# Score blocks of 64 by 64 tokens, with block-diagonal keys and values of head pairs, in a gated linear-attention and ternary feed-forward kernel

## The chip, the cores and the metric

The kernel runs on one core of a Trainium2 chip. The metric is device time in microseconds of one launch, median of the runs. Of the core's engines TensorE (PE in the rows; PEld is its weight load) multiplies, VectorE is DVE, ScalarE is ACT and GpSimd is POOL. SyncE (SP) only issues DMA transfers here; its rows are marked SPq. Names such as hid_a or score_b are PSUM banks.

## What is computed

x is 8 batches of 1024 tokens by 256 features, with 16 heads of 16 dimensions. Cut to what matters:

```python
xn = layernorm(x)
Q, K, V = (xn @ W.T).reshape(B, L, 16, 16)            # for Wq, Wk, Wv
g = clip(sigmoid(xn per head @ gw.T), 1e-6)
Gc = exp(clip(cumsum(log g), -30, 30)) + 1e-6
R = silu(K @ sw.T)
S = cumsum(outer(K, V) * R / Gc) * Gc                 # over tokens, per head
attn = einsum(Q, S) @ Wo.T
ffn = ternary(w_proj) applied to relu(ternary(w_fc) applied to xn + low-rank term) ** 2
out = x + attn + ffn
```

The cumulative sum over tokens is computed by chunks of 128 tokens: inside a chunk as masked scores (K times Q, kept where the key's token is not later than the query's) times V * R / Gc, and across chunks by a state that is carried.

## The kernel before

Work goes by units of 256 tokens (two chunks c = 0, 1 of 128), four units (u) to a batch (b), 32 in all. Each engine has its own program, written out by hand: a `prologue()` for the start, then `slot(b, u)` 27 times, then an `epilogue()`. In a slot, `nxt` is the unit one ahead, `after` two ahead, and the front of the pipeline works three and four ahead. Engines meet through semaphores alone, and each runs its list strictly in the order written, so the order in the slots is the schedule. SP issues all steady transfers on one queue, also in its written order.

The path of a unit: x is loaded and normalised (DVE, ACT, POOL), turned by a transposing DMA (`turn_tokens`), and multiplied into queries (L2272), keys (L2294), values and gates (L2313), and hidden features (L2418, L2420), whose squares go through `projected` (L2447). Queries and keys are kept as pairs of f16 halves, high and low.

- **Scores** (L2346). The contraction of 128 rows holds two heads of 16 dimensions times the four products of high and low parts. `stack_queries` (L492, 8 transfers) writes q_diag, in which head s of a pair has its own columns and zeros below the other head; `turn_keys` (L558, one transposing transfer) and `stack_keys` (L571, 4 transfers) write k_stack. One matmul has 128 keys of a pair as weights and moves 256 columns: 128 queries for each of two heads. Four groups g of two matmuls make a chunk, in banks score_a and score_b by turns.
- **Mask** (L1829, DVE): each group of 128x512 from PSUM to SBUF, times the causal triangle. A group's bank is free only after that.
- **Values** (L2384): v_pad holds each head's weighted values beside zeros, 32 columns wide. Sixteen f32 matmuls per chunk, each 128 columns of one head's scores, go to four 32-column strips of the array, four side by side. The rows count two entries for one f32 matmul. v_pad is written by POOL, `weigh_values` (L719), twice per unit.
- **State**: `state_updates` (L2361), in the same 32-column form with 64 moving columns; DVE adds it (L1843, L1847), POOL spreads it (`diagonal_state`, L746), and `carried` (L2397) adds its part to attn_bank.
- `attn_projected` (L2462) ends a unit's output; `cumulate` (L2326) makes the running sums of log gates, with 64 moving f16 columns.

In the prologue POOL turns the feed-forward weights into ternary halves (L821, L829, L836, L842), and ACT first sums their absolute values (L1230).

## Time and profile before

| what | value |
|---|---|
| median of 3 runs | 637.78 us (637.02 to 638.42) |
| span of the profiled execution, which is also its time | 637.8 us |
| PE busy | 620.1 us (97%) |
| DVE, ACT, POOL busy | 528.7, 443.3, 387.3 us (83%, 70%, 61%) |
| DMA queue q1, share of 16 engines' time | 68.4% |
| chain that ended last, on PE | 89% |

The first and last instruction are 637.8 us apart, within 0.1 us of the median, so the sums are made against 637.8. A matmul's own duration in a row (273 ns for 256 columns) overlaps with its neighbours'; what it costs is the distance between the starts of two. The chain that ended last merges equal pieces and shows that distance.

### The profile page before, as it was taken

How to read it: one execution, taken by the hardware profiler on the slowest of the kernel's cores; microseconds unless marked ns; L12 is line 12 of the kernel's file. 1: busy time of each engine (PE TensorE's matmuls, PEld its weight loads, DVE VectorE, ACT ScalarE, POOL GpSimd, SP SyncE). 2: the span in 40 equal slices, each digit the busy share in tenths (PEclk: the TensorE clock that was granted, in tenths of full speed). 3: DMA queues.
4: the chain of work that ended last, by engine and by line, in shares of the span. 5: the costliest groups of instructions: out<-in, count | busy, mean ns of one | idle time of the engine just before them, and what ended most of it. 6: DMA issues, size and time to landing. Idle time of an engine off the chain costs nothing.

```text
span 637.8 us, 21397 instructions
## 1 busy us (share of the span) xinstructions
PE 620.1 (97%) x7710; PEld 545.8 (86%) x7710; DVE 528.7 (83%) x1241; ACT 443.3 (70%) x1036; POOL 387.3 (61%) x505
## 2 busy tenths in 40 slices
PE   7789999999999999999999999999999999999997
PEld 7667888888888888888888888888888888888886
DVE  7678978899888888898789988798988887897863
ACT  4568766677776667776666767775777766677664
POOL 4896666555656665556566565655565665666454
PEclk7689999999999999999999999999999999999999
DMA  9446656886796887866788887668887477775631
GB/s 303 104 97 107 131 106 147 136 145 131 139 147 109 141 138 130 143 133 128 121 145 132 132 146 145 125 106 136 134 143 151 117 137 131 135 130 124 115 54 51
DMA packets 190361, 83.31 MB, mean 131 GB/s; under 512 B 121888, under 2 KB 189728, under 8 KB 190256
## 3 DMA queue, kind: packets, MB, share of 16 engines
q1 hardware_dynamic: 188016, 79.32, 68.4%
q10 hardware_dynamic: 2240, 2.62, 1.3%
q8 instruction: 62, 1.02, 0.8%
q14 instruction: 43, 0.35, 0.2%
HBM read 12.43 MB, written 8.39 MB: 33 GB/s over the span
## 4 chain that ended last, share of the span: by engine, by line
PE 89%; POOL 4%; issue 2%; DMA 2%; SPq 1%; DVE 1%; ACT 1%; ACTq 0%; DVEq 0%; POOLq 0%
PE y_bank L2447 17%; PE attn_bank L2384 9%; PE hid_b L2418 8%; PE hid_a L2418 8%; PE front_b L2313 7%; PE y_bank L2462 7%; PE front_b L2272 7%; PE front_a L2294 6%; PE attn_bank L2397 4%; PE score_a L2346 4%; PE score_b L2346 4%; PE hid_b L2420 2%; PE hid_a L2420 2%; PE score_b L2361 2%; POOL sq_l L821 1%
## 5 line engine op out<-in xcount | busy, mean ns | idle before, releaser
L1871 DVE TENSOR_TENSOR sq_l<-relu_sq,sq_h 128x512 f16<-128x512 f32 x128 | 115.8, 907 | 3.7 <-ACT relu_sq L1162 2.6
L2447 PE MATMUL y_bank<-wproj_t,sq_h 128*128 128x256 f16 x504 | 117.0, 273 | 0.2 <-DVE sq_l L1871 0.2
L2447 PE MATMUL y_bank<-wproj_t,sq_l 128*128 128x256 f16 x504 | 117.0, 273 | 0.0
L1829 DVE TENSOR_TENSOR masked<-score_a,shapes_sb 128x512 f32<-128x512 f32 x128 | 88.2, 689 | 29.6 <-PE score_a L2346 29.0
L1829 DVE TENSOR_TENSOR masked<-score_b,shapes_sb 128x512 f32<-128x512 f32 x128 | 87.5, 684 | 14.0 <-PE score_b L2346 13.7
L746 POOL TENSOR_TENSOR state_diag<-state,state_mask 128x256 f32<-128x256 f32 x56 | 46.8, 836 | 70.7 <-DVE state L1847 34.3
L1153 ACT ACTIVATE sq_h<-relu_sq 128x512 f16<-128x512 f32 x128 | 79.0, 618 | 0.9
L1162 ACT ACTIVATE relu_sq<-relu_sq 128x512 f32<-128x512 f32 x128 | 78.7, 616 | 0.8 <-DVE sq_l L1871 0.7
L2418 PE MATMUL hid_b<-xt,wfc_t 128*128 128x256 f16 x512 | 73.6, 273 | 0.0
L2418 PE MATMUL hid_a<-xt,wfc_t 128*128 128x256 f16 x512 | 73.4, 273 | 0.1
L672 POOL TENSOR_SCALAR xn<-x_sb,neg_mean,rstd 128x256 f32<-128x256 f32 x64 | 42.3, 662 | 50.1 <-DVE rstd L1723 49.9
L679 POOL TENSOR_TENSOR xn<-xn 128x512 f16<-128x512 f32 x31 | 35.9, 1159 | 58.7 <-ACT xn L985 58.7
L2384 PE MATMUL attn_bank<-masked,v_pad 128*32 128x128 f32 x2048 | 68.4, 274 | 0.6 <-POOL v_pad L719 0.6
L719 POOL TENSOR_TENSOR v_pad<-vg,write 128x256 f32<-128x256 f32 x64 | 38.6, 624 | 42.8 <-DVE write L1818 42.8
L2313 PE MATMUL front_b<-wvg_h,xt 128*128 128x304 f16 x256 | 61.6, 299 | 3.1 <-DVE wvg_l L1561 2.8
L1142 ACT ACTIVATE relu_sq<-hid_b,hid_scale 128x256 f32<-128x256 f32 x128 | 53.6, 473 | 13.4 <-PE hid_b L2420 13.2
L2384 PEld LDWEIGHTS attn_bank<-masked,v_pad 128*32 128x32 f32 x2048 | 52.9, 110 | 7.2 <-issue 6.1
L1047 ACT ACTIVATE vg<-front_b 128x304 f32<-128x304 f32 x64 | 27.5, 430 | 42.1 <-PE front_b L2313 42.1
L1001 ACT ACTIVATE q<-front_b 128x512 f16<-128x512 f32 x32 | 19.1, 596 | 53.3 <-PE front_b L2272 51.8
L766 POOL TENSOR_TENSOR attn_l<-attn,attn_h 128x256 fp32r<-128x256 f32 x64 | 55.8, 874 | 0.2
L1142 ACT ACTIVATE relu_sq<-hid_a,hid_scale 128x256 f32<-128x256 f32 x128 | 52.5, 460 | 4.3 <-PE hid_a L2420 4.3
L2447 PEld LDWEIGHTS y_bank<-wproj_t,sq_h 128*128 128x128 f16 x504 | 49.3, 98 | 6.2 <-DVE sq_l L1871 0.5
(224 smaller groups left out, 1656.9 us busy)
## 6 DMA issues: line engine op xcount, KB each, us to landing
q_diag<-q SPq DMA_DIRECT2D x256, 64.0 KB, 2.8
k_stack<-k SPq DMA_DIRECT2D x128, 128.0 KB, 4.3
x_sb<-in_x SPq DMA_DIRECT2D x32, 256.0 KB, 3.2
out_y<-y_both SPq DMA_DIRECT2D x31, 256.0 KB, 3.2
relu_sq<-in_w_fc ACTq DMA_DIRECT2D x1, 1024.0 KB, 11.5
pj_nat<-in_w_proj ACTq DMA_DIRECT2D x1, 1024.0 KB, 14.2
y_both<-in_w_qk ACTq DMA_DIRECT2D x1, 512.0 KB, 5.1
w_stage<-in_w_qkvz_t SPq DMA_DIRECT2D x1, 512.0 KB, 6.7
```

What stands on the lines that cost most here:

```text
L746: nc.gpsimd.tensor_tensor(state_diag[:].rearrange("p t (g s e) -> p (t g) s e", s=2, e=HD), lanes.unsqueeze(2).to_broadcast([P, KT * 4, 2, ...
L766: nc.gpsimd.tensor_tensor(attn_l[:, u % 2, c], attn[:, c], attn_h[:, u % 2, c].bitcast(F32), ALU.subtract).then_inc(attn_l_done, 1)
L1142: last = nc.scalar.activation(relu[:, n, half], hid_bank[n][:, half], ACT.Relu, scale=hid_scale[:, 2 * q + i:2 * q + i + 1])
L1153: nc.scalar.activation(sq_h[:, q], relu[:, q % 2], ACT.Square).then_inc(sq_h_done, 1)
L1162: nc.scalar.activation(sq[:, n], relu[:, n], ACT.Square).then_inc(sq_done, 1)
L1829: nc.vector.tensor_tensor(masked[:, c, g].rearrange("p (h n) -> p h n", h=4), score_bank[g % 2][:].rearrange("p (h n) -> p h n", h=4), cau ...
L1871: nc.vector.tensor_tensor(sq_l[:, q], sq[:, n], sq_h[:, q], ALU.subtract).then_inc(sq_l_done, 1)
L2313: last = mm(front_b[:, 0:VG], part[:, at, c, t], w[:, t], start=(n == 0), stop=(n == 3 * KT - 1), skip_group_check=True)
L2346: last = mm(score_bank[g % 2][:, i * 2 * P:(i + 1) * 2 * P], k_stack[:, par, g, c, i], q_diag[:, par, 2 * g + i, :, c * P:(c + 1) * P], st ...
L2384: last = mm(attn_bank[32 * q:32 * q + 32, (c * KT + half) * P:(c * KT + half + 1) * P], v_pad[:, par, c, 8 * half + 2 * q + odd], masked[: ...
L2418: mm(place, wfc_t[:, t, j * P:j * P + P], part[:, at, :, t], start=(t == 0 and part is xt_h), stop=False)
L2447: last = mm(out_part(b, u, c), part[:, q, at:at + P], wproj_t[:, 2 * q + i], start=(q == i == n == 0 and (c == 0 or last_of_all(b, u))), s ...
```

## The change

Scores are cut into causal blocks of 64 keys. The weights of one matmul now hold 64 keys of the two heads of a pair, block-diagonal (k_diag: keys of one head beside zeros, below them zeros beside the keys of the other), and q_stack has both heads' dimensions in its rows with the queries moved once. Rows are stacked four apart (`n:P:PART`). Per chunk there are three waves in place of four groups: waves 0 and 1 multiply keys 0 to 63 by all 128 queries (4 matmuls of 128 columns each), wave 2 multiplies keys 64 to 127 by queries 64 to 127 alone (8 matmuls of 64 columns). The quarter in which all keys are later than the queries is not computed. The values' weights (v_pair) hold both heads of a pair, 64 keys each; half of a head's rows must change their partitions for it. POOL's `keep_rows` writes those that stay, DVE's new `move_rows` those that move, and v_all keeps plain weighted values for the state update. Every engine's order is written anew.

```diff
@@ -65,7 +65,10 @@
 STATES = NU * CH - 1
 PART = 4
 XBUFS, TBUFS = 6, 5
-Q_DMAS, K_DMAS = 2 * PART, PART
+Q_DMAS, K_DMAS = PART, 2 * PART
+SUB = P // 2
+WAVES = 3
+ROW = CH * KT * 2 * P
...
         k_tok16 = sb("k_tok16", [P, 2, CH, D], F16)
-        k16 = sb("k16", [P, 2, CH, KT, P], F16)
-        k_stack = sb("k_stack", [P, 2, PAIRS // KT, CH, KT, P], F16)
-        q_diag = sb("q_diag", [P, 2, PAIRS, 2, UNIT], F16)
+        k16 = sb("k16", [P, 2, CH * KT * 2, 2, SUB], F16)
+        k_diag = sb("k_diag", [P, 2, PAIRS // KT * ROW + SUB], F16)
+        q_stack = sb("q_stack", [P, 2, PAIRS, UNIT], F16)
...
-        v_pad = sb("v_pad", [P, 2, CH, H, 2 * HD])
-        masked = sb("masked", [P, CH, 4, 512])
+        v_all = sb("v_all", [P, 2, CH, D])
+        v_pair = sb("v_pair", [P, 2, CH, 2, PAIRS, 2 * HD])
+        masked = sb("masked", [P, CH, WAVES, 512])
+        causal_two = sb("causal_two", [P, P])
...
+        def keys_of(par, g, c, t, s):
+
+            at = g * ROW + ((c * KT + t) * 2 + s) * P
+            return k_diag[:, par, at:at + P]
...
-                    sp.wait_ge(score_full, upto(pb, pu, 4 * CH, 4 * CH - 1))
-                if b == 0 and u < 2:
-                    sp.wait_ge(q_cleared[par], 2)
-                for s in range(2):
-                    for n, part in enumerate((0, 1, 0, 1)):
-                        rows = slice(32 * n + HD * s, 32 * n + HD * (s + 1))
-                        sp.dma_start(q_diag[rows, par, :, s, :],
-                                     q16[64 * s:64 * s + 64, part]).then_inc(q_stacked[par], 16)
+                    sp.wait_ge(score_full, upto(pb, pu, WAVES * CH, WAVES * CH - 1))
+                for n, part in enumerate((0, 1, 0, 1)):
+                    sp.dma_start(q_stack[n:P:PART, par], q16[:, part]).then_inc(q_stacked[par], 16)
...
-                sp.dma_start(k16[:].rearrange("p s c t n -> p (s c t) n"),
-                             k_tok16[:].rearrange("p s c d -> p (s c d)"),
-                             transpose=True).then_inc(k_turned[u % 2], 16)
+                if first_of_all(b, u):
+                    sp.wait_ge(k_cleared, 2)
+                for h in range(2):
+                    sp.dma_start(k16[:].rearrange("p s (x h) z n -> p (s x) h z n", h=2)[:, :, h, 0],
+                                 k_tok16[SUB * h:SUB * h + SUB].rearrange("p s c d -> p (s c d)"),
+                                 transpose=True).then_inc(k_turned[u % 2], 16)
...
-                for n, part in enumerate((0, 0, 1, 1)):
-                    sp.dma_start(k_stack[32 * n:32 * n + 32, par], k16[:, part]).then_inc(k_stacked[par], 16)
+                    sp.wait_ge(score_full, upto(pb, pu, WAVES * CH, WAVES * CH - 1))
+                if b == 0 and u < 2:
+                    sp.wait_ge(k_cleared, 2)
+                for s in range(2):
+                    to = k_diag[:, par, SUB * s:SUB * s + PAIRS // KT * ROW].rearrange("p (g n) -> p g n", n=ROW)
+                    for n, part in enumerate((0, 0, 1, 1)):
+                        sp.dma_start(to[SUB * s + n:SUB * s + SUB:PART],
+                                     k16[64 * s:64 * s + 64, part]).then_inc(k_stacked[par], 16)
 
             def slot(b, u):
-                nxt, prev, after = unit_after(b, u, 1), unit_after(b, u, -1), unit_after(b, u, 2)
-                load(*unit_after(b, u, 4))
+                nxt, after = unit_after(b, u, 1), unit_after(b, u, 2)
+                stack_queries(*after)
                 turn_tokens(*unit_after(b, u, 3))
                 stack_keys(*after)
+                store(*unit_after(b, u, -2))
+                spread_totals(*after)
                 turn_decays(*nxt)
+                load(*unit_after(b, u, 5))
                 turn_z(*after)
-                spread_totals(*after)
-                store(*unit_after(b, u, -2))
-                stack_queries(*unit_after(b, u, 3))
                 turn_keys(*unit_after(b, u, 3))
...
-                    pool.wait_ge(attn_full, carried_upto(pb, pu, CH - 1))
-                val = vg[:, par, c, 0:D].rearrange("p (g s e) -> p g s e", s=2, e=HD)
-                fac = heads_bc(write[:, par, c], HD).rearrange("p (g s) e -> p g s e", s=2)
+                    pool.wait_ge(updates_done, upto(pb, pu, 1, 0))
+                val = vg[:, par, c, 0:D].rearrange("p (h e) -> p h e", e=HD)
+                nc.gpsimd.tensor_tensor(v_all[:, par, c].rearrange("p (h e) -> p h e", e=HD), val,
+                                        heads_bc(write[:, par, c], HD), ALU.mult).then_inc(v_all_done, 1)
+
+            def keep_rows(b, u):
+
+                if not exists(b):
+                    return
...
+                    pool.wait_ge(values_done, upto(pb, pu, CH, CH - 1))
                 if b == 0 and u < 2:
                     pool.wait_ge(v_cleared[u], 1)
-                nc.gpsimd.tensor_tensor(v_heads(par, c, 0, H), val, fac, ALU.mult).then_inc(v_pad_done, 1)
+                for s in range(2):
+                    rows = slice(SUB * s, SUB * s + SUB)
+                    nc.gpsimd.tensor_tensor(block_of(par, rows, s, s), heads_of(vg[:, par, :, 0:D], rows, s),
+                                            weights_of(par, rows, s), ALU.mult).then_inc(v_kept_done, 1)
+
+                    pool.wait_ge(v_kept_done, upto(b, u, 2, s))
...
             def slot(b, u):
                 nxt, prev, after = unit_after(b, u, 1), unit_after(b, u, -1), unit_after(b, u, 2)
                 diagonal_state(*nxt, 0)
-                attn_high(b, u, 1)
+                attn_low(b, u, 0)
                 residual(*prev)
+                attn_low(b, u, 1)
+                sums_before(*after)
                 normalise(*unit_after(b, u, 4), 0)
-                attn_low(b, u, 1)
+                normalise(*unit_after(b, u, 4), 1)
+                xt_low(*unit_after(b, u, 4))
                 diagonal_state(*nxt, 1)
-                normalise(*unit_after(b, u, 4), 1)
-                sums_before(*after)
-                xt_low(*unit_after(b, u, 4))
+                keep_rows(*after)
                 weigh_values(*after, 0)
+                attn_high(*nxt, 0)
                 weigh_values(*after, 1)
-                attn_high(*nxt, 0)
+                attn_high(*nxt, 1)
                 split_decay(*after)
-                attn_low(*nxt, 0)
...
             def prologue():
-                rstd_guess(0, 0)
-                causal_taken()
-                ident_taken()
-                columns_high(0)
-                first_high()
-                columns_high(1)
                 fc_sums(0)
                 fc_sums(1)
+                rstd_guess(0, 0)
+                proj_sums()
+                columns_high(0)
                 rstd_guess(0, 1)
-                keys(0, 0)
-                keys_high(0, 0)
-                queries_high(0, 0)
-                queries_full(0, 0)
+                first_high()
                 values_high()
                 z_norms()
+                columns_high(1)
...
+            def move_rows(b, u, s):
+
+                if not exists(b):
+                    return
+                par, rows = u % 2, slice(SUB * s, SUB * s + SUB)
+                to = slice(SUB * (1 - s), SUB * (1 - s) + SUB)
+                dve.wait_ge(write_done, upto(b, u, 1, 0))
...
+                nc.vector.tensor_tensor(block_of(par, to, s, 1 - s), heads_of(vg[:, par, :, 0:D], rows, 1 - s),
+                                        weights_of(par, rows, 1 - s), ALU.mult).then_inc(v_moved_done, 1)
+
             def mask(b, u, c, g):
...
-                nc.vector.tensor_tensor(masked[:, c, g].rearrange("p (h n) -> p h n", h=4),
-                                        score_bank[g % 2][:].rearrange("p (h n) -> p h n", h=4),
-                                        causal_sb.unsqueeze(1).to_broadcast([P, 4, P]), ALU.mult).then_inc(mask_done, 1)
+                width = P if g < KT else SUB
+                shape = causal_two[:, 0:width].unsqueeze(1).to_broadcast([P, 512 // width, width])
+                nc.vector.tensor_tensor(masked[:, c, g].rearrange("p (h n) -> p h n", n=width),
+                                        score_bank[(WAVES * c + g) % 2][:].rearrange("p (h n) -> p h n", n=width),
+                                        shape, ALU.mult).then_inc(mask_done, 1)
...
-                if started(upto(b, u, 4 * CH, 4 * c + g) - 2):
-                    pe.wait_ge(mask_done, upto(b, u, 4 * CH, 4 * c + g) - 2)
-                for i in range(2):
-                    last = mm(score_bank[g % 2][:, i * 2 * P:(i + 1) * 2 * P],
-                              k_stack[:, par, g, c, i],
-                              q_diag[:, par, 2 * g + i, :, c * P:(c + 1) * P], start=True, stop=True)
+                if started(upto(b, u, WAVES * CH, WAVES * c + g) - 2):
+                    pe.wait_ge(mask_done, upto(b, u, WAVES * CH, WAVES * c + g) - 2)
+                to = score_bank[(WAVES * c + g) % 2]
+                if g < KT:
+                    for i in range(PAIRS // KT):
+                        last = mm(to[:, i * P:(i + 1) * P], keys_of(par, i, c, g, 0),
+                                  q_stack[:, par, KT * i + g, c * P:(c + 1) * P], start=True, stop=True)
+                else:
+                    for t in range(KT):
+                        for i in range(PAIRS // KT):
+                            at = (t * (PAIRS // KT) + i) * SUB
+                            last = mm(to[:, at:at + SUB], keys_of(par, i, c, t, 1),
+                                      q_stack[:, par, KT * i + t, c * P + SUB:(c + 1) * P], start=True, stop=True)
                 last.then_inc(score_full, 1)
...
-                pe.wait_ge(mask_done, upto(b, u, 4 * CH, 4 * CH - 1))
+                pe.wait_ge(mask_done, upto(b, u, WAVES * CH, WAVES * CH - 1))
+                pe.wait_ge(v_all_done, upto(b, u, CH, CH - 1))
...
-                pe.wait_ge(mask_done, upto(b, u, 4 * CH, 4 * c + 3))
+                pe.wait_ge(mask_done, upto(b, u, WAVES * CH, WAVES * c + WAVES - 1))
                 for half in range(KT):
-                    for odd in range(2):
+                    for later in range(2):
                         for q in range(4):
-                            pair = KT * q + half
-                            at = (pair % 2 * 2 + odd) * P
-                            last = mm(attn_bank[32 * q:32 * q + 32, (c * KT + half) * P:(c * KT + half + 1) * P],
-                                      v_pad[:, par, c, 8 * half + 2 * q + odd],
-                                      masked[:, c, pair // 2, at:at + P],
-                                      start=(c == half == odd == 0), stop=False, skip_group_check=True)
+                            at = (c * KT + half) * P
+                            if later:
+                                cols = (4 * half + q) * SUB
+                                place, moving = slice(at + SUB, at + P), masked[:, c, KT, cols:cols + SUB]
+                            else:
+                                place, moving = slice(at, at + P), masked[:, c, half, q * P:q * P + P]
+                            last = mm(attn_bank[32 * q:32 * q + 32, place], v_pair[:, par, c, later, 4 * half + q], moving,
+                                      start=(c == half == later == 0), stop=False, skip_group_check=True)
                 last.then_inc(values_done, 1)
```

PE, one steady slot, before: from the end of the hidden layer to the first score groups.

```order
L2420 MATMUL hid_b<-z_stack,rank_w 128x256
L2384 MATMUL attn_bank<-masked,v_pad 32x128 x16
L2361 MATMUL score_b<-v_pad,k_tok 32x64 x16
L2384 MATMUL attn_bank<-masked,v_pad 32x128 x16
L2397 MATMUL attn_bank<-q_t,state_diag 128x128 x2
L2272 MATMUL front_b<-xt,wqk 128x256 x12
```

PE, the same place in the changed kernel (L2460 values, L2432 state updates, L2471 carried, L2388 cumulate, L2334 queries, L2356 keys).

```order
L2460 MATMUL attn_bank<-masked,v_pair 32x64 x4
L2432 MATMUL score_b<-v_all,k_tok 32x64 x16
L2471 MATMUL attn_bank<-q_t,state_diag 128x128 x2
L2388 MATMUL front_a<-log,causal 128x64
L2334 MATMUL front_b<-xt,wqk 128x256 x12
L2460 MATMUL attn_bank<-masked,v_pair 32x128 x4
L2460 MATMUL attn_bank<-masked,v_pair 32x64 x4
L2460 MATMUL attn_bank<-masked,v_pair 32x128 x4
L2460 MATMUL attn_bank<-masked,v_pair 32x64 x4
L2356 MATMUL front_a<-wqk,xt 128x256 x12
```

The second chunk's values, which stood right behind the state updates, now stand alone between the queries and the keys; half of the value matmuls are 64 columns wide.

SP, one steady slot, before (from the token load on):

```order
L466 DMA x_sb<-in_x 128x2x256
L504 DMA_TRANSPOSE xt<-xn 128x8x128
L571 DMA k_stack<-k 32x4x512 x4
L531 DMA_TRANSPOSE turned_halves<-decay_halves 128x8x128
L519 DMA_TRANSPOSE z_stack<-z 128x2x128
L546 DMA totals<-chunk_sums 128x1x32
L477 DMA out_y<-y_both 128x2x256
L492 DMA q_diag<-q 16x8x256 x8
L558 DMA_TRANSPOSE k<-k_tok 128x8x128
```

SP, one steady slot of the changed kernel:

```order
L505 DMA q_stack<-q 32x4x512 x4
L516 DMA_TRANSPOSE xt<-xn 128x8x128
L590 DMA k_diag<-k 16x4x1024 x8
L494 DMA out_y<-y_both 128x2x256
L558 DMA totals<-chunk_sums 128x1x32
L543 DMA_TRANSPOSE turned_halves<-decay_halves 128x8x128
L483 DMA x_sb<-in_x 128x2x256
L531 DMA_TRANSPOSE z_stack<-z 128x2x128
L573 DMA_TRANSPOSE k<-k_tok 128x8x64 x2
```

Eight query transfers became four, four key transfers eight (of twice the elements in sum, zeros included), and one transposing transfer two of half the rows.

ACT, the first work behind the table load, before, and then in the changed kernel (L1278 sums the feed-forward weights, L1019 and L1021 begin a unit's reciprocal deviation, L1287 sums the projection's weights, L1251 takes the high half of the query and key columns):

```order
L973 ACTIVATE log_var<-var_eps 128x2
L975 ACTIVATE guess<-log_var 128x2
L1087 ACTIVATE causal<-shapes_sb 128x128
L1208 ACTIVATE ident<-shapes_sb 128x128
L1209 ACTIVATE ident<-shapes_sb 128x128
L1203 ACTIVATE wqk<-q_t 128x2x256
```

```order
L1278 ACTIVATE sq_h,fc_scale<-relu_sq 128x256 x8
L1019 ACTIVATE log_var<-var_eps 128x2
L1021 ACTIVATE guess<-log_var 128x2
L1287 ACTIVATE y_both,pj_scale<-pj_nat 128x1024 x2
L1251 ACTIVATE wqk<-q_t 128x2x256
```

The first unit's guess now stands behind the sums of the feed-forward weights.

## Rows read from the trace of the kernel before

**Rows 1.** Page, parts 1 and 2: busy time; granted TensorE clock in tenths.

```profile
PE 620.1 (97%) x7710; PEld 545.8 (86%) x7710; DVE 528.7 (83%) x1241; ACT 443.3 (70%) x1036; POOL 387.3 (61%) x505
...
PEclk7689999999999999999999999999999999999999
```

**Rows 2.** Busy time by stretch: window, length, PE, PEld, DVE, ACT, POOL, clock, DMA share, GB/s.

```profile
52.00:137.60 85.60, 84.25 (x1125) 73.37 (x1117) 71.81 (x168) 62.20 (x147) 52.58 (x73) 1.00 0.63 127
...
285.50:433.00 147.50, 147.50 (x1883) 130.78 (x1875) 128.48 (x295) 105.92 (x248) 89.08 (x118) 1.00 0.76 132
```

**Rows 3.** Timeline of PE: state updates of two units four apart: start, length.

```profile
285.47 0.34 PE L2361 MATMUL score_b<-v_pad,k_tok 128*32 128x64 f32 x11
...
359.43 0.28 PE L2361 MATMUL score_b<-v_pad,k_tok 128*32 128x64 f32 x6
```

**Rows 4.** Chain that ended last, one unit: start, length, what.

```profile
303.33 1.01 PE attn_bank L2384 x32
304.34 0.45 PE score_b L2361 x32
304.78 0.87 PE attn_bank L2384 x32
305.65 0.64 PE attn_bank L2397 x4
...
308.48 0.45 PE attn_bank L2397 x4
308.93 0.03 PE front_a L2326
...
311.14 0.22 PE score_a L2346 x2
```

**Rows 5.** Timeline of PE in the prologue: f16 matmuls with 128x128 weights each.

```profile
35.58 0.22 PE L2208 MATMUL y_bank<-ident,sq_h 128*128 128x128 f16 x1 [2.52 <-issue]
...
36.02 0.19 PE L2326 MATMUL front_a<-log,causal 128*128 128x64 f16 x1
36.05 0.22 PE L2208 MATMUL attn_bank<-ident,sq_h 128*128 128x128 f16 x1
```

**Rows 6.** Weight loads of the scores: busy us, mean ns of one.

```profile
L2346 PEld LDWEIGHTS score_b<-q_diag,k_stack 128*128 128x128 f16 x256 | 24.7, 98 | 5.2 <-DVE masked L1829 1.0
```

**Rows 7.** Timeline of SP's issues, one unit: start, length.

```profile
320.45 2.54 SPq L571 DMA_DIRECT2D k_stack<-k  x4
...
324.77 1.17 SPq L519 DMA_TRANSPOSE z_stack<-z  x1
327.71 0.53 SPq L546 DMA_DIRECT2D totals<-chunk_sums  x1
...
328.98 5.16 SPq L492 DMA_DIRECT2D q_diag<-q  x8
...
338.58 1.91 SPq L571 DMA_DIRECT2D k_stack<-k  x3
```

**Rows 8.** One line's DMA issues: ns min/median/max.

```profile
L558 SPq DMA_TRANSPOSE k<-k_tok x32: 1245/1272/2722, 20.1 to 595.3; - x32
```

**Rows 9.** DMA share and rate of a stretch in which the key stack is written.

```profile
28.90:31.40 2.50, 2.50 (x27) 2.00 (x27) 1.72 (x10) 1.08 (x4) 2.50 (x4) 0.79 0.95 201
```

**Rows 10.** Page, part 5: mask (DVE) and weighted values (POOL).

```profile
L1829 DVE TENSOR_TENSOR masked<-score_a,shapes_sb 128x512 f32<-128x512 f32 x128 | 88.2, 689 | 29.6 <-PE score_a L2346 29.0
...
L719 POOL TENSOR_TENSOR v_pad<-vg,write 128x256 f32<-128x256 f32 x64 | 38.6, 624 | 42.8 <-DVE write L1818 42.8
```

**Rows 11.** Timeline of POOL in the prologue.

```profile
9.15 1.10 POOL L672 TENSOR_SCALAR xn<-x_sb,neg_mean,rstd 128x256 f32<-128x256 f32 x2 [4.40 <-DVE rstd L1723]
...
17.37 3.63 POOL L829 TENSOR_SCALAR sq_h<-relu_sq,fc_scale 128x256 f16<-128x256 f32 x4 [3.50 <-DVE fc_inv L1582]
```

**Rows 12.** Timeline of ACT in the prologue: the first sum of feed-forward weights.

```profile
13.38 0.42 ACT L1230 ACTIVATE sq_h<-relu_sq 128x256 f16<-128x256 f32 x1 [0.74 <-DMA relu_sq<-in_w_fc]
```

**Rows 13.** Timeline of PE in the prologue: the first unit's values.

```profile
51.52 1.08 PE L2384 MATMUL attn_bank<-masked,v_pad 128*32 128x128 f32 x32 [0.59 <-POOL v_pad L719]
```

870 lines of the change are left out of this document (442 added, 428 removed).

## The prediction

> **What bounds the kernel now.** I read the page's busy line and clock line first [rows 1]: PE is busy 97% of the span, and after the first slices the clock stands at full. Busy PE is not yet a bound, since matmuls overlap in that line, so the second view is the busy time by stretch [rows 2]: from 285.5 to 433 us PE has no idle time at all, and between 52 and 137.6 only 1.35 us. The third is the chain that ended last [rows 4], in which one PE piece follows the next without a wait. Two units four apart start 359.43 - 285.47 = 73.96 us apart [rows 3], so a unit takes 18.49 us, and that is the sum of PE's pieces. Whatever PE work disappears from the slot shortens the kernel, as long as the others keep up: DVE works 128.48/147.50 x 18.49 = 16.1 us per unit, POOL 11.2 us, and the DMA engines 0.76 x 18.49 = 14.1 us [rows 2]. The first 51.5 us are another regime: the first values wait for POOL [rows 13].
>
> **Scores.** Before, 16 matmuls of 256 columns per unit at 0.22/2 = 0.11 us [rows 4], 1.76 us. After, 16 matmuls of 128 columns and 16 of 64, each with its own 128x128 f16 weights. The prologue has the first form: eight steps from 35.58 to 36.02, 0.055 us each [rows 5]. Of the second form it has one at a time: `cumulate`, 64 columns, is followed 0.03 us later by a matmul with other weights [rows 5], and the same 0.03 stands in the steady chain [rows 4]. So 16 x 0.055 + 16 x 0.03 = 1.36 us, a gain of 0.40 us per unit. Eight of the short form in a row are nowhere in this trace. If each needs the step of the 128-column form after all, 0.055 us, the gain is 0.00; it cannot be much below 0.03. I take 0.03, because in both places the next weights had to be loaded beside a 64-column matmul.
>
> **Values.** Before, 0.87 us per chunk for 32 entries of 128 columns, 0.027 each [rows 4]. The state updates are the same 32-column form with 64 columns: 0.45 us for 32 entries, 0.014 each [rows 4]. After, a chunk is 16 entries of each: 0.435 + 0.225 = 0.66 us. Gain 0.21 per chunk, 0.42 us per unit.
>
> **What the new order costs on PE.** The f32 work on 32-column strips now stands in two blocks per unit, the second chunk's values alone between queries and keys. Entering such a block costs 1.01 - 0.87 = 0.14 us, and leaving it at most 0.64 - 0.45 = 0.19 us [rows 4], part of which may be the carried matmul's own f32 weights. A second block costs 0.14 to 0.33 us; I take 0.24. PE's balance is 0.40 + 0.42 - 0.24 = 0.58 us per unit, a unit of 17.91 us, and 32 x 0.58 = 18.6 us in all.
>
> **DVE and POOL.** DVE loses two masks of 0.69 us per unit and gains two `move_rows` of 256 elements on half the partitions: no such row exists; a mask of 512 elements (0.69) bounds it from above, nothing from below, and 0.4 is near half. DVE then needs 16.1 - 1.38 + 0.8 = 15.5 of 17.9 us, the share it has now. POOL gains two `keep_rows`, at most 0.62 each as the 256-element product of today [rows 10]: 12.4 of 17.9 us. Both stay below PE. The waits for v_kept, v_moved and v_all come in the slot before the one that reads them. Behind `keep_rows`, which waits for the write factors, stand only `weigh_values`, `attn_high` and `split_decay` on POOL, which need them or come later. I charge zero to 5 us over the whole run for brushes between neighbours, and take 1.3.
>
> **SP's queue and the transfers.** This cover is thin. From 320.45 to 338.58 the queue stands still only between the end of the issue at 324.77 and the one at 327.71, 1.77 us [rows 7]; 16.36 us are issuing. The number of plain issues stays 15 (8 + 4 + 3 before, 4 + 8 + 3 after), and they cost by count, not by bytes: 5.16/8 = 0.645 us for 64 KB, 2.54/4 = 0.635 us for 128 KB. But the keys' transpose becomes two issues. If each costs what the whole does, 1.27 us [rows 8], SP needs 17.6 us of a unit of 17.9. If it divides, nothing is added; I take the whole, the nearest row. The bytes of the key stack double, 0.5 MB more per unit, at the 201 GB/s of a stretch full of such writes 2.6 us [rows 9]: the DMA engines would be busy 16.7 of 17.9 us. In the new slot `stack_keys` stands ahead of `spread_totals`, which waits for a sum that PE's `cumulate` makes early in its slot; so the keys are issued some 6 us ahead of their first score group and have room for a landing that is late by one or two.
>
> **The start.** ACT now sums the feed-forward weights before the first unit's guess. Their data come at 13.38 us and eight sums follow [rows 12], and POOL puts the first 3.63 us of ternary work, at 17.37, ahead of the first xn, which stood at 9.15 [rows 11]. The first unit's tokens are some 12 us later. Most of this does not reach the end, since the first values waited for POOL, at 51.52 [rows 13]. But POOL gets work in front of those values that it had done in idle time: 1.10 for xn [rows 11], two subtractions of 512 elements at twice 0.62, two `keep_rows` at 0.62, and a copy of about 1: 5.8 us. PE in turn takes other work ahead of them, one hidden quarter, queries and keys of unit 2, 10 x 0.11 + 12 x 0.11 + 12 x 0.11 = 3.7 us. 2 us remain. SP has to fill the pipeline at 17.6 us per unit, and I add 2 for that: +4 us, between 0 and 8. The end I leave as it is.
>
> **The sum.** 637.8 - 18.6 + 4 + 1.3 = 624.5 us.
>
> **The rivals.**
> (A) The forecast, 624.5; 618 to 630 with the bounds above.
> (B) The start costs nothing and PE is the only bound: 637.8 - 18.6 = 619.
> (C) SP's queue or the landings hold PE a little, a unit of 18.2: (18.2 - 17.9) x 29 = 8.7 us more, 633. For it: 0.3 us of room. Against it: a queue with less than PE's period catches up.
> (D) A 64-column matmul with 128x128 weights steps by 0.055: 0.025 x 16 x 32 = 12.8 us more, 637, no change. Against it: the 0.03 of [rows 4, 5].
> (E) Slower: SP's queue becomes the bound. Its place is `turn_keys`, now two issues, and the stack of twice the bytes behind them. It decides once SP needs more than 18.4 us, 2.0 more than now: two transposes at the 2.72 us that the longest took [rows 8] would do it, or a DMA load over 18.4 us, where I have 16.7. A unit of 19.0 gives 623.2 + 1.1 x 29 = 655.
> (F) Slower: weights in a row do not hide behind short matmuls. A load's record lasts 98 ns [rows 6]; if that were the step, 32 x 0.098 = 3.14 us stand for 1.36, and 624.5 + 1.78 x 32 = 681. Against it: loads of the same 98 ns step by 55 ns in [rows 5].
> The Trainium skill ("TensorE: Matmul & The Clock Gate", section "Back-to-back issue gap") speaks for something like F: it gives about 81 ns for a 128-column matmul in a stream with weight loads, and calls the 56 ns of a lone one too low. By that page, an estimate, the scores would take at least 32 x 0.081 = 2.6 us per unit, some 40 us more than I have, and the kernel would be near 664. The eight in a row of [rows 5] step by 55 ns, so I go by the trace.
>
> **How the numbers follow.** A 0.56, B 0.10, C 0.14, D 0.07, E 0.10, F 0.03. A measurement of this kernel can tell about 0.2% from no change, 1.3 us. Faster: A, B, C and a part of D, 0.82. Within 0.2%: the middle of D, 0.04. Slower: E, F and the rest of D, 0.14. The range from 616 to 638 takes in A to D and leaves out E, F and a few in a hundred below.
>
> **What would show it.** In the profile of the changed kernel: score groups of four 128-column matmuls and of eight 64-column ones both stand as pieces of 0.22 to 0.24 us in the chain (0.44 for the second is D); values of a chunk stand as 0.66 us, 0.80 where they enter; PEld's idle time ahead of the values' loads doubles; units four apart are 71.6 us apart; the first values start near 57 us. If SP's list of waits is nearly empty and PE waits for key, query or token transfers, it is C or E. If the period is right and the end late, my start was too cheap. The forecast is wrong as a whole if DVE or POOL, not PE, stands in the chain.

## The result, and the profile after

| | before | after |
|---|---|---|
| median, runs side by side | 638.26 us (636.64 to 642.45, 20 runs) | 641.41 us (637.86 to 647.18, 20 runs) |
| ratio | | 1.0045, 95% interval 1.0028 to 1.0061 |
| span of the profiled execution | 637.8 us | 636.1 us |

The change makes the kernel 0.45% slower, 3.2 us, where 624.5 us was forecast. The profile of after is that of the fastest of its 20 runs: its time is 637.86, 1.8 us above its span, and in every later run here the time lies 1.8 us above the span. So the profiled execution of before, with a span of 637.8, took some 639.6, which is 1.3 above its median, while that of after lies 3.5 below its own. My sum started at 637.8, which is within 0.5 us of the median and 1.8 too low for the profile. A comparison of the two profiles therefore makes the change look better than it is: -1.7 us, where the medians say +3.2.

The page of after, parts 1, 2 (clock) and 3 (the plain queue: packets, MB, share of the 16 DMA engines), and the shares of the chain that ended last:

```profile
PE 602.5 (95%) x8222; PEld 525.4 (83%) x8222; DVE 557.2 (88%) x1239; ACT 442.0 (69%) x1036; POOL 427.8 (67%) x569
...
PEclk8799999999999999999999999999999999999999
...
q1 hardware_dynamic: 172816, 96.16, 61.9%
...
PE 64%; DVE 8%; issue 7%; SPq 7%; POOL 6%; DMA 4%; ACT 2%; DVEq 0%; ACTq 0%; POOLq 0%
```

PE is busy 17.6 us less than before [rows 1], so its work did become smaller. But it has a chain in which it holds 64% only; issue time, SP's queue and POOL have come in. The busy time by stretch (columns as in [rows 2]):

```profile
57.00:146.00 89.00, 82.10 (x1199) 69.91 (x1200) 74.81 (x167) 59.47 (x137) 59.71 (x81) 1.00 0.65 155
146.00:290.80 144.80, 143.95 (x2024) 126.50 (x2019) 135.38 (x295) 105.73 (x249) 97.21 (x135) 1.00 0.68 166
290.80:437.00 146.20, 144.36 (x2027) 126.50 (x2020) 136.33 (x295) 105.91 (x250) 97.66 (x135) 1.00 0.70 164
437.00:583.00 146.00, 144.45 (x2024) 126.43 (x2016) 135.25 (x291) 106.13 (x250) 99.67 (x136) 1.00 0.67 166
```

In the first 89 us PE stands idle for 6.9 us, where before it had 1.35 idle us in a like stretch [rows 2]; behind that, 0.85 to 1.8 us per 8 units, where before had none up to 433 us and 1.3 in the last 150. The share of the DMA engines is not the cause: it fell from 0.76 to 0.70, though the bytes rose. DVE works 93% of the stretch.

The timeline of PE (start, length, what) gives the starts of the state updates of units 1, 6 and 31:

```profile
57.28 0.32 PE L2432 MATMUL score_b<-v_all,k_tok 128*32 128x64 f32 x8
...
146.00 0.29 PE L2432 MATMUL score_b<-v_all,k_tok 128*32 128x64 f32 x8
...
601.30 0.29 PE L2432 MATMUL score_b<-v_all,k_tok 128*32 128x64 f32 x8
```

The same points stood before at 52.41, 137.56 and 601.52. Between the two profiles that makes +4.87 us up to the first, +3.57 over five units, -8.66 over the 25 units of the loop (455.30 for 463.96 us, 18.21 us a unit for 18.56), -1.61 for unit 32 and +0.09 behind it: -1.7 in all, as the spans say. The loop gives back 0.35 us a unit, not 0.58, and 8.4 us go before it settles.

SP's timeline of one unit (same columns) shows what is new:

```profile
296.53 0.57 SPq L483 DMA_DIRECT2D x_sb<-in_x  x1
...
298.46 2.53 SPq L573 DMA_TRANSPOSE k<-k_tok  x2
301.08 3.15 SPq L505 DMA_DIRECT2D q_stack<-q  x4
304.33 1.27 SPq L516 DMA_TRANSPOSE xt<-xn  x1
305.70 5.05 SPq L590 DMA_DIRECT2D k_diag<-k  x8
310.80 1.05 SPq L494 DMA_DIRECT2D out_y<-y_both  x1
311.95 0.54 SPq L558 DMA_DIRECT2D totals<-chunk_sums  x1
312.60 1.28 SPq L543 DMA_TRANSPOSE turned_halves<-decay_halves  x1
313.93 1.21 SPq L483 DMA_DIRECT2D x_sb<-in_x  x1
315.23 1.17 SPq L531 DMA_TRANSPOSE z_stack<-z  x1
316.50 3.93 SPq L573 DMA_TRANSPOSE k<-k_tok  x2
```

From one `turn_keys` to the next, 298.46 to 316.50, there is no pause: 18.04 us of work, where [rows 7] had 16.36 and a pause. Added up from the traces over the 25 slots of the loop (issues with the gaps of 0.05 to 0.1 us between them), the queue's work is 17.9 us a slot on average and up to 19.6, with 0.3 of pauses; before it was 16.2 with 2.3 of pauses. The lists of waits (us in total, times, longest) follow, SP's and then POOL's. SP's is nearly empty in the loop, and on POOL the sums over earlier units now wait for their totals, 29 times (before: 10.6 us in all):

```profile
SPq L516 <- POOL xn L703: 21.1, 1, 21.1
...
SPq L573 <- DVE k_tok L1782: 5.0, 8, 1.5
...
SPq L558 <- DVE chunk_sums L1822: 1.7, 2, 1.1
```

```profile
POOL attn_h L801 <- DVE attn L1923: 68.7, 29, 3.1
POOL before L719 <- DMA totals<-chunk_sums: 54.6, 29, 5.6
```

The wait of 21.1 us is one, in the prologue. Before, the loop's waits were 34.5 us in 28 for `chunk_sums` and 20.7 in 18 for `z`.

PE's own list of waits names no transfer in the loop, only DVE, in small pieces. The chain of after shows how a late queue still reaches PE, here ahead of one of the two longest units, 19.6 us:

```profile
441.68 3.96 DMA totals<-chunk_sums
...
445.71 0.23 POOL before L719
...
449.22 0.69 DVE masked L1894
...
449.95 0.40 PE score_b L2410 x4
```

The new order has the totals of log gates behind the eight key writes and the store on the queue. When they land late, POOL's sums are late, then DVE's work on them and the masks behind it, and PE waits for a mask. The other long unit, 19.5 us, has the same chain.

### The profile page after: what moved, and what is told of

Read it like the earlier page. It is cut to its first block, busy times and chain, and to the rows that moved or that the text cites. A ratio compares the mean times of both kernels' runs of the same rounds, so it can differ in the third digit from the quotient of the medians.

```text
span 636.1 us, 22704 instructions
## 1 busy us (share of the span) xinstructions
PE 602.5 (95%) x8222; PEld 525.4 (83%) x8222; DVE 557.2 (88%) x1239; ACT 442.0 (69%) x1036; POOL 427.8 (67%) x569
## 3 DMA queue, kind: packets, MB, share of 16 engines
q1 hardware_dynamic: 172816, 96.16, 61.9%
## 4 chain that ended last, share of the span: by engine, by line
PE 64%; DVE 8%; issue 7%; SPq 7%; POOL 6%; DMA 4%; ACT 2%; DVEq 0%; ACTq 0%; POOLq 0%
PE y_bank L2521 12%; PE hid_a L2492 6%; PE front_b L2375 6%; PE hid_b L2492 6%; PE y_bank L2536 6%; PE attn_bank L2460 6%; PE front_a L2356 5%; PE front_b L2334 5%; PE attn_bank L2471 3%; SPq L590 3%; DMA totals<-chunk_sums 3%; DVE masked L1894 2%; PE score_b L2410 2%; DMA relu_sq<-in_w_fc 2%; PE score_a L2410 2%
## 5 line engine op out<-in xcount | busy, mean ns | idle before, releaser
L1936 DVE TENSOR_TENSOR sq_l<-relu_sq,sq_h 128x512 f16<-128x512 f32 x128 | 111.1, 870 | 2.4 <-ACT sq_h L1201 1.8
L1210 ACT ACTIVATE relu_sq<-relu_sq 128x512 f32<-128x512 f32 x128 | 80.2, 628 | 41.5 <-DVE sq_l L1936 41.4
L801 POOL TENSOR_TENSOR attn_h<-attn,ones 128x256 fp32r<-128x256 f32 x64 | 56.8, 888 | 70.3 <-DVE attn L1923 68.7
L1894 DVE TENSOR_TENSOR masked<-score_b,causal_two 128x512 f32<-128x512 f32 x96 | 65.5, 683 | 2.3 <-PE score_b L2410 1.5
L1894 DVE TENSOR_TENSOR masked<-score_a,causal_two 128x512 f32<-128x512 f32 x96 | 65.2, 680 | 0.7 <-PE score_a L2410 0.3
L2460 PEld LDWEIGHTS attn_bank<-masked,v_pair 128*32 128x32 f32 x2048 | 45.2, 109 | 12.5 <-issue 11.9
L2460 PE MATMUL attn_bank<-masked,v_pair 128*32 128x128 f32 (+1 forms) x2048 | 55.3, 249 | 0.1
L2521 PEld LDWEIGHTS y_bank<-wproj_t,sq_l 128*128 128x128 f16 x504 | 49.3, 98 | 5.0
L2492 PEld LDWEIGHTS hid_a<-xt,wfc_t 128*128 128x128 f16 x512 | 47.7, 98 | 6.6 <-issue 1.1
L2492 PEld LDWEIGHTS hid_b<-xt,wfc_t 128*128 128x128 f16 x512 | 47.9, 98 | 5.2
```

Of the source, the lines that this page charges most:

```text
L801: nc.gpsimd.tensor_tensor(attn_h[:, u % 2, c], attn[:, c], ones[:].unsqueeze(1).to_broadcast([P, KT, P]), ALU.mult).then_inc(attn_h_done, 1)
L1210: nc.scalar.activation(sq[:, n], relu[:, n], ACT.Square).then_inc(sq_done, 1)
L1894: nc.vector.tensor_tensor(masked[:, c, g].rearrange("p (h n) -> p h n", n=width), score_bank[(WAVES * c + g) % 2][:].rearrange("p (h n) -> ...
L1936: nc.vector.tensor_tensor(sq_l[:, q], sq[:, n], sq_h[:, q], ALU.subtract).then_inc(sq_l_done, 1)
L2460: last = mm(attn_bank[32 * q:32 * q + 32, place], v_pair[:, par, c, later, 4 * half + q], moving, start=(c == half == later == 0), stop=Fa ...
L2492: mm(place, wfc_t[:, t, j * P:j * P + P], part[:, at, :, t], start=(t == 0 and part is xt_h), stop=False)
```

## The experiments

**The theories.** S: SP's queue, full since the key transpose is two issues, sets the pace of the changed loop. V: DVE, 93% busy, sets it. L: the transfers land late, though the queue has room. F: the order of the start costs time of its own. P: PE's pieces are not as short as I summed. The chain already speaks against P. One unit of it:

```profile
309.28 0.45 PE score_b L2432 x32
309.72 0.64 PE attn_bank L2471 x4
...
311.70 0.80 PE attn_bank L2460 x32
312.50 1.42 PE front_a L2356 x12
...
317.20 0.22 PE score_a L2410 x4
...
319.30 0.23 PE score_a L2416 x8
```

**One more small transfer per unit, in each kernel.** The same edit in both:

```diff
                 turn_keys(*unit_after(b, u, 3))
+                sp.dma_start(spare_in[:, nth(b, u)], shapes[0:16, 0:8]).then_inc(gates_loaded, 16)
```

> The changed kernel with one more transfer at the end of each of SP's 27 slots: 16 rows of 32 bytes into a tile that nothing reads. Theory S (SP's issue queue is the bound of the changed kernel: its trace shows SP without idle time between issues and units 18.1 to 18.2 us apart): each extra issue costs its 0.6 to 0.65 us, so 27 x 0.63 = 17 us, 655 to 661 us. Theory V (VectorE, 93% busy in the steady stretches, is the bound) and theory L (landings are late, the queue has room): nothing, 641 us within 2.

> The kernel before with the same extra transfer in each of SP's 27 slots. All theories: SP stands still for about 1.8 us per unit there, so 0.63 us more is free: 638 us within 1.5. If it costs 5 us or more, the queue already counted before the change, and theory S would be too simple.

Measured: the changed kernel 657.06 us (653.91 to 660.9, 4 runs; ratio to before 1.0268, 1.0227 to 1.0309), 15.6 above its own 641.4 (14.2 when each is taken by its ratio to before): 0.53 to 0.58 us for each of 27 issues, one whole issue each. The kernel before 641.34 (10 runs; 1.0039, 1.0012 to 1.0066), 2.3 us for the same 27. So after has no slack in this queue and before has most of 0.6 us. The first is as S expected, and V and L expected nothing of it; the second is nearly as expected (it was to be free). S stands, but this does not say what filled the queue.

**The second transpose alone, in the kernel before.**

```diff
-                sp.dma_start(k16[:].rearrange("p s c t n -> p (s c t) n"),
-                             k_tok16[:].rearrange("p s c d -> p (s c d)"),
-                             transpose=True).then_inc(k_turned[u % 2], 16)
+                for h in range(2):
+                    sp.dma_start(k16[:].rearrange("p s c t n -> p (s c t) n")[:, :, P // 2 * h:P // 2 * h + P // 2],
+                                 k_tok16[P // 2 * h:P // 2 * h + P // 2].rearrange("p s c d -> p (s c d)"),
+                                 transpose=True).then_inc(k_turned[u % 2], 16)
...
```

Those who wait for the turned keys count two transfers per unit in place of one; nothing else differs.

> The kernel before with the keys' transposing transfer cut into two of half the rows, as the change does. It prices the second transpose by itself. Theory S: 1.2 to 1.3 us more issue time per unit, which eats most of the 1.8 us of idle time: 638 to 642 us, SP's waits shrink by about 35 us in sum. If half a transpose costs half, the waits stay as they were.

Measured: 660.9 us (657.77 to 664.16, 4 runs; 1.0335, 1.0297 to 1.0373), 22 us slower. This was a miss, and the most useful one. SP's waits and PE's first:

```profile
SPq L546 <- DVE chunk_sums L1780: 22.8, 24, 3.5
...
SPq L519 <- DVE z L1801: 8.5, 11, 2.1
```

```profile
PE front_b L2273 <- DMA xt<-xn: 17.5, 16, 2.5
```

```profile
DVE stats L1681 <- DMA x_sb<-in_x: 21.3, 23, 3.0
```

The queue still waits for 22.8 + 8.5 us there, and yet PE now waits for the turned tokens, 16 times, and DVE's statistics for x, 23 times, which the kernel before did once (1.3 us) and 6 times (5.1 us). The chain of that run has one of these waits, and the timeline of the queue what lies around it:

```profile
318.63 5.25 DMA xt<-xn
...
323.93 1.48 PE front_b L2273 x12
```

```profile
318.63 1.24 SPq L504 DMA_TRANSPOSE xt<-xn  x1
319.97 3.01 SPq L572 DMA_DIRECT2D k_stack<-k  x4
323.07 1.26 SPq L531 DMA_TRANSPOSE turned_halves<-decay_halves  x1
324.60 1.17 SPq L519 DMA_TRANSPOSE z_stack<-z  x1
327.06 0.53 SPq L546 DMA_DIRECT2D totals<-chunk_sums  x1
...
328.33 6.52 SPq L492 DMA_DIRECT2D q_diag<-q  x8
334.95 2.54 SPq L559 DMA_TRANSPOSE k<-k_tok  x2
```

PE stands idle for 1.8 us until the tokens issued at 318.63 have landed. From 289 to 324.3, almost two slots, the queue has no gap of more than 0.1 us: the eight query writes took 6.4 us in each, where [rows 7] have 5.16, and the key writes 3.96 and 3.01 for 2.54. The pause, 325.8 to 327.1, comes only behind PE's wait; it stands ahead of the totals, which wait for PE's sums. In the next slot the queries follow without a wait. The landing itself is not slower than in the kernel before, 4.0 us in the median against 3.9; the issue comes late. So the queue is full for a slot or two, holds PE, and waits for PE afterwards, and its pauses in other slots do not pay for that. I had read a pause per unit as room for as much work: some 0.6 us nearly fitted, 1.27 did not. The two halves cost 2.54 together, and each 1264 ns in the median of 64, the whole's 1272.

**The same transpose taken out of the changed kernel, and DVE relieved.** Two omissions from the fifth unit on, alone and together (the counts of those who wait for the transpose are adapted):

```diff
-                for h in range(2):
+                for h in range(2 if nth(b, u) < 4 else 1):
...
```

```diff
-                nc.vector.tensor_tensor(block_of(par, to, s, 1 - s), heads_of(vg[:, par, :, 0:D], rows, 1 - s),
-                                        weights_of(par, rows, 1 - s), ALU.mult).then_inc(v_moved_done, 1)
+                if nth(b, u) < 4:
...
+                else:
+                    nc.vector.tensor_tensor(block_of(par, to, s, 1 - s)[:, 0, 0, 0:2],
...
```

> The changed kernel without the second of its two key transposes per unit from the fifth unit on (half of the keys' rows stay those of earlier units, so that the output differs): the transfer queue loses some 1.5 us of its 18 us per unit. It is the mirror of the second transpose added to the kernel before, which cost 22 us. Theory S (queue): the loop falls to TensorE's own 17.99 us per unit and the last of the start with it, time 633 to 637, and the queue shows waits again of about 1.5 us per unit. Theory V (VectorE): no change beyond 1 us, 640 to 642. Theory B: part of it, 637 to 640.

> The changed kernel with the work of VectorE's two value moves per unit (64x256, 0.52 us each) left out from the fifth unit on: they write two elements instead, so that the output differs; nothing else moves. VectorE loses 0.9 us of its 16.9 busy us per unit of 18.1. Theory S (the transfer queue is the bound of the changed kernel's loop): no change beyond 1 us, 640 to 642. Theory V (VectorE, 93 per cent busy, is what holds TensorE since the change): the loop comes down from 18.2 to 18.3 us a unit to TensorE's own 18.0, time 634 to 637. Theory B (each of the two is near the bound and delays TensorE in its turn): part of it, 638 to 640.

> Both of the two last omissions at once (second key transpose and the work of the value moves, each from the fifth unit on). Theory S: as the omission of the transpose alone. Theory V: as the omission of the moves alone. Theory B (both near their bounds): lower than either, loop at 17.99 us per unit throughout, time 631 to 635, some 3 us below the better of the two.

| | median us | ratio to before |
|---|---|---|
| one transpose | 631.59 (630.41 to 636.45, 5 runs) | 0.9900, 0.9866 to 0.9934 |
| no value moves | 640.33 (638.4 to 644.84, 10 runs) | 1.0034, 1.0010 to 1.0058 |
| both | 630.61 (628.51 to 631.87, 4 runs) | 0.9878, 0.9843 to 0.9914 |

Against after's 641.41 and 1.0045 the transpose is worth 9.3 us by the ratios and 9.8 by the medians, more than S expected. DVE's 0.9 us per unit give 0.7 to 1.1, alone or on top of the transpose, and the intervals of these pairs overlap: no gain of DVE is clear of the noise. This decides for S against V, and leaves B at most 1 us. The kernel with one transpose, its page and PE by stretch:

```profile
PE 76%; DVE 7%; issue 5%; POOL 4%; DMA 3%; SPq 3%; ACT 2%; ACTq 0%; DVEq 0%; POOLq 0%
```

```profile
57.00:146.00 89.00, 84.47 (x1250) 72.61 (x1249) 76.97 (x172) 61.14 (x140) 61.24 (x83) 1.00 0.67 160
...
290.80:437.00 146.20, 145.84 (x2062) 128.66 (x2061) 137.62 (x299) 106.43 (x251) 102.93 (x138) 1.00 0.65 159
```

PE is busy 145.84 of 146.20 us in the second, with DVE at 94% beside it: in this order DVE can be this full and hold PE for 0.4 us at most. The 25 units take 450.82 us, 18.03 each, with a cycle of 18.10, 18.10, 17.88 and 17.74 us where nothing waits, 17.96 on average. That is PE's own time for a unit; with both omissions the 25 units take 449.13, 17.97 each.

**Loads and stores on ACT's queue.**

```diff
                 stack_keys(*after)
-                store(*unit_after(b, u, -2))
                 spread_totals(*after)
                 turn_decays(*nxt)
-                load(*unit_after(b, u, 5))
```

with `store_behind` behind `z_high` and `load_ahead` behind `decay_exp` in ACT's slot, the same transfers on ACT's queue.

> The changed kernel with the steady loads of x and stores of the output issued from ScalarE's queue in place of SP's (ScalarE is 69% busy): SP has 1.2 to 1.9 us less per unit. Theory S: units fall from 18.2 to PE's own 17.9 us and the pipeline fills faster, 628 to 635 us. Theory V: VectorE does the same work, 641 us or more. Theory L: bytes and landings are the same, 641 us.

Measured: 640.43 us (12 runs; 1.0019, 1.0000 to 1.0038), 1 to 1.7 us under after, not 6 or more. Two issues less per unit, and no gain to speak of: S missed here, and V and L come nearer. DVE's waits of that kernel:

```profile
DVE stats L1737 <- DMA x_sb<-in_x: 5.3, 5, 3.4
```

In after that wait stood once, 3.5 us, ahead of the first unit, and one of these five is the same; the four in the loop make 1.9 us together. The queue has pauses again, 1.6 us a slot, and yet the 25 units take 457.35 us, 8.5 more than PE's own time. PE waits for masks there, 4.3 us in 9 and 3.3 in 4 (after: 2.2 in 6 and 2.3 in 2). So a queue with room is not enough; what holds this kernel was not found. The next runs moved the stores alone, with the start order as a second factor.

**The start order of before, and the stores alone.** `after_early` puts the order ahead of the first unit back on all engines; on POOL it reads

```diff
-                fc_highs(0)
                 normalise(0, 0, 0)
                 normalise(0, 0, 1)
                 columns_low(0)
-                fc_lows(0)
+                columns_low(1)
+                fc_highs(0)
```

> The changed kernel with one part undone: the order of the work before the first unit is put back to that of the kernel before on all engines (the first unit's tokens, keys and queries ahead of the scales and sums of later weights), with the new layouts kept. The steady loop is untouched. Theory F (the new start order costs time of its own): the first values began at 57.28 us against 52.41, and the state updates of the sixth unit at 146.0 against 137.56, though each unit's matmuls are 0.5 us shorter; with the old order the first state updates should begin at 52 to 54 us and the sixth unit's by 139 to 142, and the time falls by 3 to 6 us from 641.4, to 635.5 to 638.5. Rival (the fill is paced by the transfer queue's own work, which is the same in both orders): the first values begin earlier, but the sixth unit's start stays within 1.5 us of 146, and the time stays at 640 to 641.5.

> The changed kernel with its own start order and the output stores alone issued on ScalarE's queue, the loads of x on SyncE's. The kernel that had moved both gained 1 us of the 10 that the queue's relief can give (leaving out the second key transpose), and there x landed late (VectorE's statistics waited for it 5 times, 5.3 us). Theory X (the loads of x, issued late on ScalarE, ate the gain): the stores alone give more than both, 635.5 to 638. Rival L (a second queue that issues in the loop stretches the transposes on the first): 639.5 to 641.5, no better than both moved.

> The changed kernel with the old start order (as before) and, from there, with the output stores alone issued on ScalarE's queue; the loads of x stay on SyncE's. This takes one issue of 0.59 us per unit from a queue that is full at 18.0 to 18.2 us per unit, and leaves the loads of x where they are. Theory S (the queue's own work is the bound): the queue needs 17.5 us, below TensorE's 17.96, so that the loop reaches TensorE's floor in most units; time 2 to 5 us under the early start's 636.7: 631.5 to 634.5, and the queue shows waits again. Rival L (what held the kernel with loads and stores moved was the queue issuing later and longer beside a second one, so that freed time is lost in stretched transposes): 636 to 637.5, no gain over the early start.

> The kernel before with its output stores issued on ScalarE's queue, as the control of the same move in the changed kernel, where it was worth 2.6 to 3.5 us. In the kernel before, SyncE's queue waits between its issues and TensorE has no idle time in the loop. Theory S (the queue bounds the changed kernel alone): no gain here, 637 to 639.5. Rival (a shorter queue helps either kernel, so that the gain of the move is not the change's): 634 to 636.

| | median us | ratio to before |
|---|---|---|
| changed, old start order | 636.72 (634.62 to 641.38, 12 runs) | 0.9975, 0.9953 to 0.9997 |
| changed, stores on ACT | 637.95 (635.98 to 640.81, 10 runs) | 1.0002, 0.9979 to 1.0026 |
| changed, both | 634.09 (632.47 to 637.69, 12 runs) | 0.9938, 0.9913 to 0.9962 |
| before, stores on ACT | 638.28 (636.42 to 640.83, 12 runs) | 0.9995, 0.9975 to 1.0015 |

The order of the start costs the changed kernel 3.9 to 4.7 us, the time that F expected. The starts that F expected did not come, though. In the profiles of the changed kernels with the new order the first state updates begin at 57.0 to 59.8 us, with the old order at 54.6 to 55.2, and in those of the kernel before at 51.1 to 52.4. From there to the sixth unit it takes 88.5 to 89.6 us with the new order and 88.3 to 90.0 with the old, as the rival said, which had the queue pace the fill; with one transpose less it takes 85.9 and 86.2. So the order moves the first unit alone, and the fill goes by the queue. (Single profiles, some of a long run and some of a short one, spread by a microsecond or two.)

The stores are worth 2.4 to 3.5 us in the changed kernel and 0.4, nothing, in the one before: the relief counts only where the queue is full. With both, PE's own time is still not reached, at 18.12 us a unit, and SP waits for `chunk_sums` only 4 times, 3.7 us in all: the queue is still nearly full. Moving less seems to give more than moving both, 1.0002 against 1.0019, but the intervals overlap, and DVE's 1.9 us of waits for x in the loop would be little of it: theory X is not shown. Not varied either is the place of the totals, ahead of the key writes or the store, though the chain of after passes there.

**The second block of values undone as well.**

```diff
                 state_updates(*nxt)
+                values(*nxt, 1)
                 carried(*nxt, 0)
                 cumulate(*after)
                 queries_t(*unit_after(b, u, 3))
-                values(*nxt, 1)
```

> The changed kernel with the old start order, the stores on ScalarE's queue, and in the loop the second chunk's values put back behind the state updates, so that TensorE has one block of f32 strip work per unit and not two. Theory P (TensorE is the bound again once the queue is relieved): entering and leaving a block cost 0.14 to 0.33 us per unit, so the time falls from 634.1 to 626 to 631. Rival M (the second chunk's values then stand ahead of the masks that VectorE, 93 per cent busy, makes for them, and TensorE waits for those): the entry is saved and lost again in waits for the masks, 634 to 640.

Measured: 635.1 us (634.4 to 637.61, 9 runs; 0.9947, 0.9925 to 0.9969), no better than the kernel without this edit (634.09, 0.9938), though PE's work is shorter: its chain has 0.66 for the second chunk's values, without the entry. In 437 us PE is busy 429.6, the other 434.7. PE's waits name the masks first, here and then in the kernel without this edit:

```profile
PE score_b L2424 <- DVE masked L1908: 5.6, 18, 0.6
```

```profile
PE score_b L2424 <- DVE masked L1908: 2.0, 6, 0.4
```

The lists are of whole runs, and of the longest of nine against the shortest of twelve; the idle time of PE in those 437 us is 7.4. P is excluded, which expected 626 to 631, and rival M's time and waits came: the second block, which I charged as a loss, gives DVE time for the masks. With the queue relieved, DVE comes next.

## Why the prediction was wrong, point by point

**PE's work: right.** Four 128-column scores take 0.22 and eight of 64 columns 0.23 to 0.25 us in the chain; a chunk's values 0.80 us with the entry, as said. The second block costs 0.80 - 0.66 = 0.14 going in and 1.42 - 12 x 0.11 = 0.10 coming out, the 0.24 that I took, and the idle time of PEld ahead of the values' loads nearly doubled as said, from 7.2 to 12.5 us. PE's unit is 17.96 us by the cycle of the kernel with one transpose, 18.49 before: 0.53 where I had 0.58. The Trainium skill ("TensorE: Matmul & The Clock Gate", section "Back-to-back issue gap") gives about 81 ns per 128-column matmul in a stream with weight loads; these rows step by 55 ns, and by 29 for 64 columns, so the page's figure does not hold for this kernel. D and F fall.

**SP's queue: the step that failed.** I had "SP needs 17.6 us of a unit of 17.9", 16.36 + 1.27. The median issue was as I took it, 1265 ns for a half. Two things were not. First, the queue's work has a spread that a median and a single slot hide: the two halves took 2.53 in one slot and 3.93 in the next, x's load 0.57 and 1.21, all in the rows above, and 12 of the loop's 23 loads of x took over 1 us, before none. The average was 17.9 us a slot, just under PE's 17.96, with slots up to 19.6. Second, "a queue with less than PE's period catches up" is false here: such a queue has no room left to make good a long slot, and where it has pauses, in the kernel before, the added transpose still cost 22 us. I priced the step at 2 us, in the start, and at part of the 1.3; taking the transpose out again gave 9.3 to 9.8 us. My limit of 18.4 us for E was the same error, made twice: it was the period before, 18.49, where PE's new one was 17.9, and the loss began below it. And of `stack_keys` ahead of `spread_totals` I had counted only what the keys gain; POOL's waits for the totals are now 54.6 us.

C and E were this mechanism; they had 0.24 between them, and C's time, 633, was too low because it took the rest of the sum as right. In the rows above the issue of a transposing DMA holds the queue 1.17 to 1.28 us and that of a plain one mostly 0.54 to 0.65. The Trainium skill ("Advanced Engine Details and Errata", section "X-Bar Transpose (TRN2)") calls transposes on trn2 as fast as regular DMAs; that is told of the moving of data, which no run here compares, and on the queue they are not.

**The start: mis-sized.** I had +4. The first values did start near 57. But the sixth unit starts at 146.0, where 137.56 + 4 - 5 x 0.58 = 138.7 was forecast. With PE's own gain of 2.65 us in five units, the start costs 11.1 us in the profile in place of 4: 4.9 up to the first state updates and 6.2 in the fill. The old order brings the first 2.7 forward (54.60 for 57.28, both single profiles), one transpose less makes the fill 2.8 shorter. The other 5.6 us stay open.

**DVE: mis-sized, of little consequence until the queue is relieved.** I had 15.5 us of work per unit; it is 136.33/146.20 x 18.1 = 16.9. The masks fell as said (176 to 131 us), but some small operations grew. In the steady loop, groups of after (busy, mean ns):

```profile
L1748 DVE TENSOR_SCALAR neg_mean<-moments 128x2 f32<-128x2 f32 x24 | 30.9, 1287 | 0.0
L1879 DVE TENSOR_TENSOR v_pair<-vg,write 64x256 f32<-64x256 f32 x48 | 24.8, 516 | 1.5
```

The first has two elements per partition and took 441 ns on the average of the whole kernel before and 1046 after; what holds it was not tried. The moves at 516 ns were 0.4 in my sum.

**The DMA engines: wrong.** I had them at 16.7 of 17.9 us, from a stretch full of key stack writes. They are at 0.70, which is 12.7 of 18.1 us. The number of bytes did not say how long they are busy.

**The sum with what was measured,** for the profiles, which it must meet since its terms are taken from them: 639.6 as the profiled time of before (637.8 + 1.8); PE's own gain 32 x 0.53 = -17.0; the start +8.4 + 5 x 0.53 = +11.1 in the profile, the loop's stall 455.3 - 25 x 17.96 = +6.3, against 1.7 before: +4.6; the ends -1.5 + 2 x 0.5 = -0.5, together 637.8 for 637.86 measured. Of the 13.4 us from 624.5 to there, the start is 7.1, the loop 3.3, PE's work 1.6 and the base 1.8. The median run of after is 3.5 us above its profile, and why is not shown; its runs also vary more than those of before, 9.3 us between the shortest and the longest against 5.8, which would fit a queue that is full and whose issues vary.

## What to carry to other kernels

Count an in-order issue queue as an engine: its work per period with its spread, not with medians, and the time between issues with it. A pause in one slot does not make good what the queue was late with in another; price an added issue by adding it to the kernel before, at its place. When the matmul engine's work shrinks by 3%, list every engine and queue that is close to the new period before you book the gain (here SP's queue with 17.6 of 17.9 us and DVE with 16.9 of 17.96), and relieve them together: the transpose, the stores, the start order and DVE's masks came one after the other, and the best kernel with the right output, 634.1 us, books 4 of the 17 us. The old start order and one transpose per unit were not tried together.

## What was not expected of the hardware

A transposing DMA of half the rows holds its queue as long as the whole, 1264 to 1272 ns in the median, with single ones at 2.0 to 2.7 us. Eight f16 matmuls of 64 columns with 128x128 weights each take 0.23 us: their weight loads, records of some 98 ns [rows 6], do hide. The bytes of the key stack doubled, in rows of twice the length, and yet the share of the DMA engines' time, page part 3, fell from 68.4% with 79 MB to 61.9% with 96 MB. The query writes became half as many in rows of twice the length in the same change, so which of the two lowered it is open.
